# Decoder layer on one core: other PSUM banks in head and tail, head weights turned early, part of the last experts on ScalarE

## What is computed

```python
x = layernorm(x + attn(x, W_attn, W_proj))          # 16 heads of 8; causal; polymax instead of softmax
x = layernorm(x + xattn(x, ctx, WQ, WK, WV, WO, bO)) # 16 heads of 64; softmax over 64 keys
x = layernorm(x + moe(x, router_w, router_b, expert_w))
# polymax(s) = (s**2 + 1 if s > 0 else -s/100 + 1 if s >= -100 else 0) / 1000
# moe: softmax over 16 experts, the 6 best rescaled to sum 1 are the gates,
#      out = sum over all 16 experts of (x @ expert_w[e]) * gate[:, e], plus 1e-10 terms
```

## Time and profile before

| | |
|---|---|
| median of 3 runs | 1014.57 us (1012.44 to 1014.77) |
| profiled execution, its own time | 1011.26 us |
| its span, first to last instruction | 1009.5 us |
| PE busy | 955.2 us (95%) |
| DVE busy | 890.6 us (88%) |
| ACT busy | 768.7 us (76%) |
| POOL busy | 434.3 us (43%) |
| mean granted TensorE clock | 0.986 |

### The profile page before, as it was taken

How to read it: one execution, slowest core, us unless ns; L and a number is a source line. 1 busy time by engine, 2 the same in 40 slices (tenths; PEclk the granted TensorE clock), 3 DMA queues, 4 the chain that set the end, 5 groups by cost and what they waited for, 6 DMA issues and landing times.

```text
span 1009.5 us, 47204 instructions
## 1 busy us (share of the span) xinstructions
PE 955.2 (95%) x18136; PEld 843.0 (84%) x18136; DVE 890.6 (88%) x2824; ACT 768.7 (76%) x1606; POOL 434.3 (43%) x906
## 2 busy tenths in 40 slices
...
DMA packets 41882, 21.19 MB, mean 21 GB/s; under 512 B 18912, under 2 KB 40928, under 8 KB 41824
## 3 DMA queue, kind: packets, MB, share of 16 engines
...
...
## 4 chain that ended last, share of the span: by engine, by line
PE 66%; DVE 17%; issue 11%; ACT 3%; DVEq 1%; POOL 1%; DMA 0%; ACTq 0%; SPq 0%; POOLq 0%
PE ps L447 61%; DVE sums L888 4%; PE ps L572 4%; DVE allowed L852 3%; DVE p L864 2%; DVE stats L805 1%; DVE residual L888 1%; ACT prob L764 1%; DVE mv L811 1%; DVE best L911 1%; PE ps L595 1%; DVE ps L859 1%; DVEq L354 0%; ACT qm L636 0%; DVE left L920 0%
## 5 line engine op out<-in xcount | busy, mean ns | idle before, releaser
L888 DVE SCALAR_TENSOR_TENSOR sums<-ps,gate,sums 128x128 f32<-128x128 f32 x896 | 239.9, 340 | 18.5 <-PE ps L447 17.7
L996 POOL TENSOR_TENSOR p<-p,rowinv 128x1024 f32<-128x1024 f32 x64 | 121.8, 1904 | 219.1 <-DVE rowinv L841 219.0
L447 PE MATMUL ps<-wo_sb,oT 128*128 128x128 f32 x1024 | 127.5, 278 | 0.6 <-issue 0.6
L447 PEld LDWEIGHTS ps<-wo_sb,oT 128*128 128x128 f32 x1024 | 121.1, 192 | 5.4 <-issue 1.0
L636 ACT ACTIVATE v<-ps 128x512 f32<-128x512 f32 x128 | 76.3, 598 | 50.2 <-PE ps L447 45.2
L447 PE MATMUL ps<-ex_hi,x2T_hi 128*128 128x512 f32 x256 | 110.4, 431 | 3.3 <-POOL x2T_lo L978 3.1
L636 ACT ACTIVATE oT<-ps 128x512 f32<-128x512 f32 x128 | 69.6, 597 | 45.7 <-PE ps L447 45.1
L756 ACT ACTIVATE x<-residual,shift,rstd 128x128 f32<-128x128 f32 x192 | 83.7, 484 | 26.9 <-POOL shift L991 17.5
L447 PE MATMUL ps<-ex_lo,x2T_hi 128*128 128x512 f32 x256 | 101.7, 397 | 0.0
L447 PE MATMUL ps<-ex_hi,x2T_lo 128*128 128x512 f32 x256 | 101.5, 396 | 0.0
L852 DVE SCALAR_TENSOR_TENSOR allowed<-ps,const 128x512 f32<-128x512 f32 x128 | 87.1, 681 | 15.2 <-ACT relu L659 13.6
(11 more groups left out here) (119 smaller groups left out, 2675.6 us busy)
## 6 DMA issues: line engine op xcount, KB each, us to landing
...
```

What stands on the lines that cost most here:

```text
L447: return pe.matmul(o, l, r, start=start, stop=stop)
L888: done = V.scalar_tensor_tensor(after, ps(f"FF{4 * r + q}")[:, C * e:C * e + C], gate[:, r, 4 * q + e:4 * q + e + 1], before, ALU.mult, AL ...
L996: G.tensor_tensor(weights, weights, rowinv[:, r].unsqueeze(2).broadcast_to([P, H, T]), ALU.mult).then_inc(p2_ready, 1)
```

## The change

Five things are changed; the turns (`ORDER`, and `JOBS` but for the heads) stay as they are.

1. A table `OTHER_BANK` gives single jobs of single tiles another bank, in the head (tiles counted from 0) and in the tail (from -1). `ps` and `banks_of` get the tile as a second argument.
2. The lists `FIRST` and `LAST` are in another order on all engines. In the head V, K and Q of tile 0 come first, then heads1, and heads2 directly behind the first scores. In the tail the attention of the last tiles comes earlier and the experts of the tiles -6 to -4 later.
3. At the start w_attn and the constants are loaded through ScalarE's queue, wk, the context, wv and wq follow the first columns on SP's, and TensorE runs four matmuls on zeros (`WARM`).
4. For the last three tiles (`SHARED`) the fourth quarter of the experts, weigh3, is not done by VectorE. ScalarE scales the eight slices (`scale3`), GpSimd adds them in two instructions (`gather3`), and VectorE adds the result to its sum (`join3`), which writes the residual.
5. Waits for the end of a tile's sum go through `wait_summed`.

```diff
-    ("FF3", "B2", 0), ("FF7", "B5", 0), ("heads0", "P0", None), ("heads1", "P1", None), ("heads2", "P2", None),
+    ("FF3", "B2", 0), ("FF7", "B5", 0), ("heads0", "P0", None), ("heads1", "P0", None), ("heads2", "P0", None),
...
+OTHER_BANK_FIRST = """
...
+    S1_0@0=B0 S1_0@1=B1 S1_0@2=B1 S1_0@3=B0 S1_1@0=B3 S1_1@1=B2 S1_1@2=B7 S1_1@3=B6 S1_1@4=B6 S1_1@5=B6 S1_2@0=B4 S1_2@1=B4
+    S1_2@2=B3 S1_2@3=B7 S1_2@4=B7 S1_2@5=B0 S1_3@0=B1 S1_3@1=B6 S1_3@2=B2 S1_3@5=B4 Y@1=B6 Y@2=B1 Y@3=B3 Y@4=B3 Y@5=B7 PR@0=B3
...
+    X2T@1=B5 LG@0=B2 FF4@0=B4 FF1@0=B5 FF5@0=B3 FF6@0=B4 FF3@0=B5 FF7@0=B2 heads0@0=P1 heads1@0=P3 heads2@0=P3
+"""
+OTHER_BANK_LAST = """
...
+    AC1@-4=P3 AC1@-3=P0 AC1@-2=P0 AC1@-1=P2 WO0@-4=B3 WO0@-3=B3 WO0@-2=B5 WO0@-1=B3 X2T@-5=B5 X2T@-4=B1 X2T@-3=B2 X2T@-2=B1
+    X2T@-1=B6 LG@-5=B6 LG@-3=B2 LG@-2=B1 LG@-1=B0 FF0@-6=B0 FF0@-5=B2 FF0@-4=B2 FF0@-3=B0 FF0@-2=B5 FF0@-1=B3 FF4@-6=B5 FF4@-4=B3
+    FF4@-3=B2 FF4@-1=B2 FF1@-6=B7 FF1@-5=B6 FF1@-4=B4 FF1@-3=B7 FF1@-2=B3 FF5@-6=B4 FF5@-5=B4 FF5@-4=B7 FF5@-3=B5 FF5@-2=B6
...
 FIRST = {
...
     "PE": """
-        Q@0 K@0 S1_0@0 S1_1@0 S1_2@0 S1_3@0 V@0 heads1@0 heads2@0 heads0@0 K@1 Y@0 Q@1 V@1 PR@0 S1_0@1 S1_1@1 S1_2@1 S1_3@1 V@2 K@2
-        K2_2@0 K2_3@0 K2_1@0 Q@2 K2_0@0 Y@1 S1_0@2 S1_1@2 S1_2@2 S1_3@2 PR@1 X1T@0 Q2_0@0 K@3 Q2_2@0 Q2_3@0 Q2_1@0 V@3 S2_0@0 Q@3
...
+        V@0 K@0 Q@0 heads1@0 S1_0@0 S1_1@0 S1_2@0 S1_3@0 heads2@0 Q@1 heads0@0 V@1 K@1 S1_0@1 Y@0 S1_1@1 S1_2@1 S1_3@1 Q@2 PR@0 V@2
+        K2_0@0 K@2 S1_0@2 S1_1@2 K2_1@0 S1_2@2 S1_3@2 Q@3 K@3 K2_2@0 Y@1 X1T@0 K2_3@0 V2_0@0 Q2_2@0 Q2_3@0 Q2_0@0 Q2_1@0 S1_0@3 PR@1
...
     "POOL": """
-        next_x_hi@0 next_x_lo@0 next_x_hi@1 next_x_lo@1 context_hi@0 context_lo@0 root1@0 next_x_hi@2 next_x_lo@2 experts_lo@0
+        next_x_hi@0 next_x_lo@0 next_x_hi@1 context_hi@0 context_lo@0 next_x_lo@1 next_x_hi@2 next_x_lo@2 next_x_hi@3 next_x_lo@3
...
 LAST = {
...
     "PE": """
-        K2_1@-1 Q2_2@-1 Q2_0@-1 PT1b@-2 PT1a@-2 Q2_1@-1 FF0@-4 AC0@-2 FF4@-4 Q2_3@-1 V2_1@-1 AC1@-2 S2_0@-1 X2T@-3 FF5@-4 FF1@-4
-        V2_2@-1 WO0@-2 S2_1@-1 FF6@-4 FF2@-4 FF3@-4 FF7@-4 WO1@-2 LG@-3 V2_3@-1 V2_0@-1 FF4@-3 PT0a@-1 FF3@-3 PT1a@-1 FF7@-3 FF0@-3
-        FF5@-3 FF1@-3 PT1b@-1 FF2@-3 FF6@-3 X2T@-2 PT0b@-1 FF5@-2 LG@-2 FF1@-2 AC0@-1 FF0@-2 FF4@-2 AC1@-1 WO0@-1 WO1@-1 FF2@-2
-        FF6@-2 FF7@-2 FF3@-2 X2T@-1 LG@-1 FF0@-1 FF4@-1 FF1@-1 FF5@-1 FF3@-1 FF2@-1 FF6@-1 FF7@-1
+        FF2@-5 Q2_0@-1 AC0@-2 S2_0@-1 X2T@-4 PT1b@-2 V2_1@-1 S2_1@-1 LG@-4 PT1a@-2 FF3@-5 V2_3@-1 FF7@-5 AC1@-2 WO0@-2 WO1@-2 FF4@-4
+        FF0@-4 V2_0@-1 FF1@-4 FF5@-4 V2_2@-1 FF2@-4 X2T@-3 FF6@-4 LG@-3 PT0a@-1 PT0b@-1 FF7@-4 FF3@-4 PT1a@-1 AC0@-1 FF4@-3 FF7@-3
+        FF0@-3 FF1@-3 FF3@-3 FF5@-3 WO0@-1 FF6@-3 PT1b@-1 FF2@-3 X2T@-2 AC1@-1 LG@-2 WO1@-1 FF4@-2 FF0@-2 FF3@-2 FF7@-2 FF1@-2 FF5@-2
+        FF2@-2 FF6@-2 X2T@-1 LG@-1 FF3@-1 FF4@-1 FF0@-1 FF1@-1 FF5@-1 FF7@-1 FF6@-1 FF2@-1
...
     "DVE": """
-        weigh0@-3 weigh1@-3 var3@-4 weigh2@-3 weigh3@-3 logits@-2 gate0@-2 gate1@-2 gate2@-2 gate3@-2 gate4@-2 gate5@-2 gate6@-2
-        gate7@-2 gate8@-2 stats3@-3 gate9@-2 gate10@-2 weigh0@-2 var3@-3 weigh1@-2 attended@-1 stats2@-1 var2@-1 weigh2@-2 weigh3@-2
-        logits@-1 gate0@-1 stats3@-2 gate1@-1 gate2@-1 gate3@-1 gate4@-1 gate5@-1 gate6@-1 gate7@-1 gate8@-1 var3@-2 gate9@-1
-        gate10@-1 weigh0@-1 weigh1@-1 weigh2@-1 weigh3@-1 stats3@-1 var3@-1
+        gate10@-3 stats3@-4 weigh0@-3 var3@-4 weigh1@-3 weigh2@-3 logits@-2 gate0@-2 gate1@-2 gate2@-2 gate3@-2 gate4@-2 gate5@-2
+        join3@-3 gate6@-2 gate7@-2 attended@-1 gate8@-2 stats3@-3 gate9@-2 stats2@-1 gate10@-2 var2@-1 var3@-3 weigh0@-2 weigh1@-2
+        weigh2@-2 logits@-1 gate0@-1 join3@-2 gate1@-1 gate2@-1 gate3@-1 gate4@-1 gate5@-1 gate6@-1 gate7@-1 gate8@-1 gate9@-1
+        stats3@-2 var3@-2 gate10@-1 weigh0@-1 weigh1@-1 weigh2@-1 join3@-1 stats3@-1 var3@-1
...
-def banks_of(job):
+def banks_of(job, tile):
...
+    bank = OTHER_BANK.get((job, tile), BANK[job]) if isinstance(tile, int) else BANK[job]
+    n = int(bank[1:] or 0)
+    return {"": (), "P": (2 * n, 2 * n + 1), "B": (n,)}[bank[:1]]
...
-            sp.dma_start(w_attn_sb[:], w_attn).then_inc(attn_in, 16)
-            sp.dma_start(const[:], consts).then_inc(const_in, 16)
-            for dst, src, arrived in zip(heads_ld, (wq_t, wk_t, wv_t), heads_in):
-                sp.dma_start(dst, src).then_inc(arrived, 16)
+            sp.dma_start(heads_ld[1], wk_t).then_inc(heads_in[1], 16)
             load(cT, ctx_t, cT_in, 0)
+            sp.dma_start(heads_ld[2], wv_t).then_inc(heads_in[2], 16)
+            sp.dma_start(heads_ld[0], wq_t).then_inc(heads_in[0], 16)
...
+            for _ in range(WARM):
+                mm(pairs[0][:, 0:P], rows_of_zeros[:, 0:P], rows_of_zeros[:, 0:P])
             pe.wait_ge(attn_split, 1)
...
+            nc.scalar.dma_start(w_attn_sb[:], w_attn).then_inc(attn_in, 16)
+            nc.scalar.dma_start(const[:], consts).then_inc(const_in, 16)
...
+            def scale_last(tile, q):
+
+                act.wait_ge(share_steps, SHARE_STEPS * (tile + 1))
+                wait(act, extra_ready, shared_index(tile))
+                for r in range(NR):
+                    wait_full(act, f"FF{4 * r + q}", tile)
+                    for e in range(4):
+                        last = nc.scalar.activation(scaled_out[:, r, e], ps(f"FF{4 * r + q}", tile)[:, C * e:C * e + C], ACT.Copy, scale=gate[:, r, 4 * q + e:4 * q + e + 1])
+                    last.then_inc(emptied[f"FF{4 * r + q}"], 1)
...
+            def join(tile, q):
+
+                dve.wait_ge(extra_ready, shared_index(tile) + 1)
+                for r in range(NR):
+                    wait_emptied(dve, f"FF{4 * r + q - 1}", tile)
+                wait(dve, normed[3], tile)
+                V.tensor_tensor(residual[3][:], sums[:], extra[:], ALU.add).then_inc(joined, 1)
...
+            def gather(tile, q):
+
+                for r in range(NR):
+                    wait_emptied(pool, f"FF{4 * r + q}", tile)
+                wait(pool, joined, shared_index(tile))
+                G.tensor_tensor(scaled_out[:, :, 0:2], scaled_out[:, :, 0:2], scaled_out[:, :, 2:4], ALU.add).then_inc(halves_added, 1)
+                pool.wait_ge(halves_added, shared_index(tile) + 1)
+                G.tensor_tensor(extra[:], scaled_out[:, :, 0], scaled_out[:, :, 1], ALU.add).then_inc(extra_ready, 1)
```

291 lines of the change are left out of this document (164 added, 127 removed).

## The result

The changed kernel takes 1001.17 us (median of 4 runs, 1000.19 to 1002.19) against 1014.67 in the runs of before made beside it: a ratio of 0.9869, 95% interval 0.9847 to 0.9891. Its profiled execution took 1000.19 us, with a span of 998.3 (before 1011.26 and 1009.5). One execution of head_only, an experiment further down, took 5119 us and is left out of its ratio.

The account below looks back on a forecast made before the run. TensorE and VectorE were taken as full in the loop, leaving gains only in head and tail: 0 - 6 - 3 = -9 us; 1011.3 - 9 + 2.0 (for an unprofiled run) = 1004.3, said as 1004, range 996 to 1012.

Parts of the forecast that it names:

- Head, first 28 us: Start of the kernel: no gain, bounds -3 to +2 us; scores of tile 1 start at 27.8 us against 28.0.
- The moved wait: TensorE at the start: the long wait is not removed but moves from heads1 to Q@1.
- the low part of the columns: GpSimd at the start: the low part of tile 1's columns, which Q@1 needs, is done at about 23.2 us.
- Head, 28 to 142.5 us: Rest of the head before the loop: -6 us, taking 4 of 8.7 and 2 of 5.8 us TensorE idle time.
- The turns: Middle of the kernel, the loop: already full, its order, banks and work left alone, so unchanged.
- Tail: From 877.8 us to the end: -3 us, in three steps that together make -2.6.
- Step 1: Tail up to the last softmax: TensorE jobs move behind S2_1@-1; -2 us, bounds 0 and -4.6.
- Step 2: Tail from the last softmax to attended@-1, nearly all VectorE work: net -2.4 us, taken as -2.
- Step 3: Tail from attended@-1 to the end: 25.2 us, 1.4 us longer than now.
- Scalings in front of norm2: Rival, tail: ScalarE's scalings and GpSimd's gather delay two hand-overs by 10.4 us in all; time 1017.7 us, chance 0.07.
- Gather slows VectorE: Rival, tail: VectorE stands still while GpSimd adds, three gathers costing 6 us; time 1010 us, chance 0.03.
- Only the tail gets shorter: Rival: the head's new order only trades one wait for another, leaving the tail's -3 us; time 1010.3 us, chance 0.20.

Follow-up runs that it names:

- head_only: The changed kernel's head (table, banks, loads, warm-up) with the end of the kernel before; 1006.80 us, ratio to before 0.9948.
- order_only: The changed kernel with before's loads and head-weight order and no warm-up matmuls, so only table and banks of its head remain; 996.20 us, ratio to before 0.9859.
- tail_only: The changed kernel's end, including the experts' quarter on ScalarE, with the head of the kernel before; 1003.07 us, ratio to before 0.9910.
- no_share2: The changed kernel with the fourth-quarter weighings back on VectorE, and banks and weighing order mended to avoid waits for that quarter; 1004.09 us, ratio to before 0.9931.
- scale_twice: The changed kernel with every ScalarE scaling of the last three tiles done twice, the first into a spare tile; 1001.61 us, ratio to before 0.9903.

## Why the prediction was right, step by step

The direction and the range were right, and the sum of -9 us, made on the profiled execution, was 2.1 us short of its -11.07 (1000.19 against 1011.26). The two halves were right in sign, the head in size, the tail in sign alone.

- **Head, first 28 us (0 forecast).** The moved wait was right: heads1 at 6.94 us, then 8.05 us ahead of Q@1. The scores of tile 1 start at 25.9 us, not 27.8. The step that was off is the low part of the columns at "about 23.2": it was done at 20.7, since GpSimd saw the data at 18.06 instead of 20.43. I took the arrival of one profile as fixed. SP issued the load 1.4 us sooner (at 14.75 instead of 16.17 us; over the profiles that leave it in its place the issue lies anywhere from 14.8 to 16.0), and GpSimd used the data 3.3 us after the issue instead of 4.3: 2.8 to 3.8 us in the nine profiles with the new table and the load in this place, 4.3 and 4.1 in the two with the old table. Why is not shown. That the loads on ScalarE's queue and the warm-up count nothing held in order_only.
- **Head, 28 to 142.5 us (-6).** The loop starts 6.2 us sooner in the changed kernel's profile, 3.8 to 5.5 in the four others with its head, against 142.5; head_only's ratio says 5.3. The size was right, the reason half of it at most, so the number is partly luck. I took 4 + 2 us of idle time. Of the waits that the order was aimed at, 3.7 us went (10.8 to 7.1), but 2.5 us of waits that the profile doesn't explain came, and the idle time of the whole head fell by 1.9 us (3.9 in order_only). The matmuls themselves, at the higher clock, gave 4.3 (4.0 in order_only). I read the 0.89 of the earlier trace rows and then gave it no term.
- **The turns (unchanged).** Held, within the spread of 734.2 to 737.8.
- **Tail (-3; measured -7.4, and -9.1 by tail_only's ratio).** This is the term that was mis-sized. Step 1 was -5.2 where I took -2 with a bound of -4.6: S2_1@-1 came 11.1 us earlier (66.4 us after the tail's start, 77.5 before), not up to 8, and VectorE followed. Step 2 was -3.7 instead of -2. Step 3 was right: 25.3 us against 25.2, with X2T@-1 released by weigh1@-2 at +6.3 (forecast 6.4) and the weighings 0.26 us apart. I halved the work that VectorE gives up (5 us net) because "part of it falls where VectorE isn't last"; no_share2 says all 4.9 count, and order and banks (2.5) come on top.
- **Scalings in front of norm2 (0.07).** Didn't come: a scaling starts every 0.25 us (the first of eight at 974.86, the norm behind them at 976.87), under the 0.41 from which I said it decides and under my 0.35 to 0.39, and norm2@-1 was out 4.8 us after attended@-1, not 5.9 to 6.3. The mechanism was read rightly and priced too high. scale_twice shows that it is there once the scalings double.
- **Gather slows VectorE (0.03).** Didn't come: both rows of 22 weighings take 5.77 us, 0.26 apart as in the earlier trace rows, with a gather in the middle of each. The Trainium skill (Perfetto Trace Analysis, Optimizing Scalar/DVE Operations) warns that GPSIMD and DVE share an SBUF read port, so that moving work between those two might not help. These rows don't show it, for weighings that read PSUM.
- **Only the tail gets shorter (0.20).** Ruled out by head_only, 0.9948 with 0.9968 at most.
